# The products with V of each half of the heads, done at two places of the half's eighteen steps instead of four

## What is computed

```
h = _layernorm(x) * (1 + ca) + sa
q, k, v = split(h @ qkv_w.T + qkv_b);  q, k = apply_rope(q), apply_rope(k)
attn = softmax(where(causal, q k^T * scale, -1e9))
x = x + ga * ((attn @ v) @ proj_w.T + proj_b)
h = _layernorm(x) * (1 + cb) + sb
x = x + gb * spikes(square(relu(h @ W_fc.T)) @ W_proj.T)
```

## Time and profile before

| | before |
|---|---|
| three executions, us | 456.43, 461.63, 460.37 |
| the profiled execution, us | 458.5 |
| its span in the trace, us | 456.8 |
| PE busy | 391.4 us (86%) |
| DVE busy | 322.9 us (71%) |
| ACT busy | 260.0 us (57%) |
| mean granted TensorE clock | 0.989 |

### The profile page before, as it was taken

One profiled execution on the slowest core, in us unless ns is written; L12 is line 12 of the kernel. 1 busy time (PEld: TensorE's weight loads), 2 busy tenths in 40 slices (PEclk: granted clock), 3 DMA queues, 4 the chain that ended last, 5 costly groups with the idle time before them and its releaser, 6 DMA issues.

```text
span 456.8 us, 15637 instructions
## 1 busy us (share of the span) xinstructions
PE 391.4 (86%) x6611; PEld 252.2 (55%) x6611; DVE 322.9 (71%) x722; ACT 260.0 (57%) x449; POOL 124.3 (27%) x159
## 2 busy tenths in 40 slices
PE   3768979878999998899989989999899899878882
PEld 2226755545656665576557655766466657445532
DVE  5669858957883998479965996599839845530745
ACT  7202346576577566665695568666675666477220
POOL 7725002421351143304340325133510400220210
PEclk9899999999999999999999999999999999899998
DMA  6055723242314242323324251415141410110000
GB/s 207 23 171 143 234 75 104 67 123 70 112 57 122 71 108 62 101 80 93 89 83 114 52 136 61 130 28 140 52 126 45 113 46 5 27 30 23 24 1 24
DMA packets 26048, 38.53 MB, mean 84 GB/s; under 512 B 5794, under 2 KB 20714, under 8 KB 23690
## 3 DMA queue, kind: packets, MB, share of 16 engines
q1 hardware_dynamic: 25978, 37.53, 28.7%
HBM read 26.35 MB, written 8.65 MB: 77 GB/s over the span
## 4 chain that ended last, share of the span: by engine, by line
PE 44%; DVE 17%; DMA 13%; ACT 8%; SPq 7%; issue 7%; POOL 2%; POOLq 0%; ACTq 0%; DVEq 0%
PE d_bank L448 10%; PE o_bank L519 9%; PE t_bank L501 6%; PE s_bank L468 6%; DMA den<-o_raw 5%; SPq L370 4%; DVE negmax L828 4%; DMA kf<-k_scr 3%; ACT probs L703 3%; PE a_bank L448 3%; DMA rden<-r_scr 2%; DVE rot_s L864 2%; DVE xn L844 2%; SPq L374 2%; DVE count L895 2%
## 5 line engine op out<-in xcount | busy, mean ns | idle before, releaser
L828 DVE TENSOR_REDUCE negmax<-s_bank 128x1 f32<-128x448 f32 (+7 forms) x368 | 192.0, 564 | 69.0 <-PE s_bank L474 67.5
L703 ACT ACTIVATE probs<-t_bank 128x512 f32<-128x512 f32 x288 | 163.4, 595 | 85.8 <-PE t_bank L506 79.5
L468 PE MATMUL s_bank<-kf,qf 126*64 126x448 bf16 (+7 forms) x1024 | 117.4, 292 | 18.4 <-DVE negmax L828 11.7
L501 PE MATMUL t_bank<-qf,kf 128*64 128x512 bf16 (+7 forms) x1024 | 112.8, 290 | 11.6 <-ACT probs L703 10.9
L468 PEld LDWEIGHTS s_bank<-kf,qf 126*64 126x64 bf16 x1024 | 49.7, 110 | 50.2 <-DVE negmax L828 28.5
L519 PE MATMUL o_bank<-probs,v 128*32 128x512 f32 (+7 forms) x1024 | 76.2, 416 | 0.0
L474 PE MATMUL s_bank<-causal,identb 128*64 128x64 bf16 x1024 | 72.5, 194 | 0.0
L506 PE MATMUL t_bank<-causal_t,identb 128*64 128x64 bf16 x1024 | 64.7, 195 | 0.0
L501 PEld LDWEIGHTS t_bank<-qf,kf 128*64 128x64 bf16 x1024 | 41.4, 111 | 32.0 <-ACT probs L703 14.2
L506 PEld LDWEIGHTS t_bank<-causal_t,identb 128*64 128x64 bf16 x1024 | 48.0, 111 | 9.2
L474 PEld LDWEIGHTS s_bank<-causal,identb 128*64 128x64 bf16 x1024 | 47.4, 111 | 8.4 <-issue 8.1
(11 more groups left out here) (115 smaller groups left out, 432.6 us busy)
## 6 DMA issues: line engine op xcount, KB each, us to landing
qf<-q_scr SPq DMA_DIRECT2D x15, 576.0 KB
kf<-k_scr SPq DMA_DIRECT2D x45, 192.0 KB
q_scr<-parts SPq DMA_DIRECT2D x24, 128.0 KB, 1.7
k_scr<-parts SPq DMA_DIRECT2D x24, 128.0 KB, 1.7
xa<-in_x SPq DMA_DIRECT2D x8, 256.0 KB, 4.0
o_t<-o_raw SPq DMA_DIRECT2D x60, 32.0 KB, 2.1
rden<-r_scr SPq DMA_DIRECT2D x15, 128.0 KB
out_y<-count SPq DMA_DIRECT2D x7, 256.0 KB, 7.6
```

The source lines that it names most:

```text
L468: nc.tensor.matmul(bank[C * a:C * (a + 1), col:col + keys], qf[0:KS, slot, 2 * p + a, C * i:C * (i + 1)], kf[0:KS, slot, 2 * p + a, 0:keys ...
L501: nc.tensor.matmul(bank[C * a:C * (a + 1), col:col + w], kf[0:KX, slot, 2 * p + a, C * kb:C * (kb + 1)], qf[0:KX, slot, 2 * p + a, C * kb: ...
L703: nc.scalar.activation(probs[:, v, :], t_bank[u % 2][:, :], ACT.Exp, scale=SCALE).then_inc(e_done, 1)
L828: last = nc.vector.tensor_reduce(own[:, i, p:p + len(same)], cols, AX.X, ALU.max, negate=True)
```

## The change

Two tables of places are rewritten. The blocks 0, 1 and 7 are no longer visited after slot 9 but together with 2 and 6 after slot 13; the late blocks 3 and 5 no longer after slot 0 of the next half but together with 4 after its slot 1. The order of the blocks among themselves, and with it which one starts and which one ends the sum, is as it was.

```diff
-PV_AFTER = {9: (0, 1, 7), 13: (2, 6)}
-PV_LATE = {0: (3, 5), 1: (4,)}
+PV_AFTER = {13: (0, 1, 7, 2, 6)}
+PV_LATE = {1: (3, 5, 4)}
```

## The result

The changed kernel takes 480.94 us (median of 4 executions, 477.86 to 483.54), the kernel before 458.98 us in the same comparison: a ratio of 1.046, 95% interval 1.040 to 1.052. It is 22 us slower. The forecast was 472 us with a range of 463 to 482, so the direction and the range held, and the middle was 9 us too low.

The account below looks back on a forecast made before the run. DVE was taken to pace even slots 5 to 13, PE slots 14 to 17, a DMA chain odd slots 0 to 9. Terms 7.0 + 3.6 + 0.9 + 0.6 = 12.1 us on 460.37 gave 472 us, range 463 to 482.

Parts of the forecast that it names:

- the likeliest case: Slot 13 fixed by DVE or the DMA chain, its longer visit paid, at most two clock falls: 466 to 477 us, chance 0.60.
- the rival in which the clock falls: Waits of 2.7 us before odd halves' query and key product bring half clock, 1.7 us each, six times: 478 to 486, chance 0.17.
- DVE is the pace in slots 5 to 13 of even halves: DVE busy 8.80 of 8.80 us, so slot 13 ends where it did and the removed 1.95 us become PE idle time.
- the sign: Expected in the new trace: PE idle about 1.9 us more between slots 9 and 13 of an even half, ended by DVE.
- The longer visit after slot 13 is paid in even halves: Slots 14 to 17: visit 1.71 us longer, only 0.12 us of the stretch idle, so about 1.6 us stay per even half.
- give-back of 0.2 us at the late visit: Slots 0 to 4 after an even half: PE is the pace, and one saved edge pair gives -0.2 us.
- ACT absorbs about half behind slot 13 of odd halves: Behind slot 13 of odd halves: of the visit's 1.71 us extra, ACT absorbs half, leaving +0.8 us a half.
- The saved edges: 31 fewer visits, each saving two tile-width changes of 0.10 us: 6.2 us less if PE were the bound everywhere.
- Head and tail: Halves 0, 13 and 14 put at 0, half 2 at +0.9 us, half 15 at +0.6 us.
- That PE is the pace: Slots 9 to 13: if DVE's work can go earlier, up to 6.2 us gained: 454 to 456 us, chance 0.08.
- that most is absorbed: Odd halves' shorter PE waits and slack in the `den` DMA absorb most; 5 us or less: 461 to 465 us, chance 0.15.

Follow-up runs that it names:

- DVE light: Four of five spike counts of batches 0 to 6 on 32 columns instead of 512: kernel before 455.44 us, changed kernel 470.14 us.
- the even halves alone: Kernel before with blocks 0, 1, 7 moved from after slot 9 to after slot 13 in even halves only: 470.84 us, ratio 1.024.
- The runs without falls: Changed kernel plus useless repeat products after slot 9, of blocks 0, 1, 7 (480.39 us) or of 0, 7 outside halves 13 and 15 (476.71 us).
- second profile: The kernel before, unchanged, profiled once more: span 456.3 us.
- the short copy: Changed kernel plus useless repeat products of blocks 0 and 7 after slot 9, except in halves 13 and 15: 476.71 us, ratio 1.035.
- the full copy: Changed kernel plus useless repeat products of blocks 0, 1 and 7 after slot 9 of each half: 480.39 us, ratio 1.045.

## Why the forecast was right, and where it was off

The direction and the two costs of the moved visit came out as worked out, half by half. The size did not: 12.1 us were forecast and 22.0 measured. The time lies outside the band of the likeliest case (466 to 477 us) and inside that of the rival in which the clock falls (478 to 486 us, chance 0.17). That the stated range still holds it, by 1 us, is in part luck, because the range took in only the lower part of that rival.

**DVE is the pace in slots 5 to 13 of even halves: right.** The stretch kept its length to 0.1 us while PE's work in it shrank, and with DVE light the cost of an even half fell from 1.4 to 0.5 us. PE's waits for DVE in the stretch grew by 1.4 us (0.6 to 2.0), where about 1.9 was given as the sign.

**The longer visit after slot 13 is paid in even halves: right.** 1.73 us longer (5.02 to 6.75) where 1.6 was forecast. With the give-back of 0.2 us at the late visit, 1.4 us a half was forecast, and even halves without a fall are 1.4 us longer (24.37 against 22.94). With the even halves alone and the late visits as before it is 1.65 us (24.59), where 1.6 was to be expected.

**ACT absorbs about half behind slot 13 of odd halves: right.** 0.8 us forecast, 0.63 measured (6.52 to 7.15). Counted from the start of the window, the copy of the maxima starts 0.49 us later and the ReLU 0.60 us later than before, where 0.45 and 0.55 were forecast; in half 5:

```profile
190.71 1.00 ACT L709 COPY mrow<-a_bank 8x1024 bf16<-8x1024 bf16 x1 [0.39 <-PE a_bank L488]
191.72 0.60 ACT L742 ACTIVATE relu<-d_bank 128x512 f32<-128x512 f32 x1
```

The sum over halves 4 to 12 was 7.0 for five even halves and 4 x 0.8 - 0.6 = 2.6 us for four odd ones, 9.6 us. The runs without falls gave 8.9 and 10.4 us. The saved edges are seen as well: line 519 is busy 71.5 us instead of 76.2 with 31 visits fewer, 4.7 us where 6.2 were worked out, with part of its products at half clock.

**The clock: the mis-sized term.** The forecast gave it 0 in the likeliest case and 10 us in a rival with a chance of 0.17: "if such a wait brings a stretch at half clock". It did, in both kinds of half of the profile, and the four executions have a mean clock of 0.957 to 0.969, where 13 of the kernel before have 0.984 to 0.992. The price of one was 1.7 us in the rival and 1.3 to 1.6 us in the runs. In halves 4 to 12 four falls account for 5.0 to 6.5 of the 15.4 us. The rival's place was too narrow: it counted odd halves alone, but the even halves have falls too, one with the even edit alone and one in half 8 of the changed kernel. There PE waits for DVE in several pieces (the last three are 0.50, 0.19 and 0.46 us), and the clock falls in the last of them, at 263.59:

```profile
263.60:267.00 3.40, 3.22 (x24) 1.36 (x28) 3.32 (x13) 1.01 (x2) 0.51 (x1) 0.50 0.47 120
```

What argued against it, "only one wait did this", was weak evidence, because between 40 us and the end the kernel before has only two waits over 1.5 us, 2.90 us in half 0 and 1.55 us in half 14, and one of the two brought a fall.

**Head and tail: too small.** I had put halves 1 to 3 at 1.9 us together, halves 13 and 14 at 0 and 15 at 0.6 us. The part behind half 12 grew from 98.7 us (96.7 in the second profile) to 103.6 us, and the part before half 4 from 141.1 (143.2) to 146.1 us. PE's waits there were not worked out one by one. Between the first profile of before and that of the changed kernel it is 25.0 - 15.1 = 9.9 us. Both parts hold falls, seven in the changed kernel and three and two in the profiles of before; at 1.3 to 1.6 us each, four or five more would be 5 to 8 us (an estimate). One of the seven follows a wait of 2.54 us in half 2 for the `kf` DMA. How much is the moved work itself stays open; the head differs by 2 us between two profiles of the same kernel.

**The rivals on the other side fell.** That PE is the pace (454 to 456 us) and that most is absorbed (461 to 465 us) are refuted by the 480.94 us and by the stretches. The part of the forecast that the late edit is worth 0.2 us a visit was not confirmed in the times.

## What to carry to other kernels

An engine at 86% busy is not the pace everywhere. Cut one steady period at the points where the full engine changes, and read a moved piece of work as free where it leaves a stretch that another engine fills (or that ends at a DMA chain), and as paid where it arrives. Then ask what the engine does in the time that the work left behind: if it is TensorE, a wait may cost more than itself, because here most waits of 2.3 to 2.8 us, and some shorter ones, were followed by half clock.

## What the runs showed of the hardware

At the second query and key products of the changed kernel, waits of PE of 2.3 to 2.8 us were followed by 3.41 us at half clock in four cases of five, and one of 1.7 us was not. In half 8 a row of waits of 0.2 to 0.5 us was. The wait of 1.55 or 1.56 us in half 14 was followed by a fall in the first profile of before and in that of the changed kernel, and not in the second profile of before. So the length of a wait alone did not tell whether the clock would fall. A fall cost 1.3 to 1.8 us. Useless matmuls in such waits kept the clock at full speed over nine halves (1.00 against 0.97), and the kernel with the short copy was 4.2 us faster than the one with none; with the full copy the total stayed the same (480.39 against 480.94 us). The Trainium skill ("TensorE: Matmul & The Clock Gate", Part 1) describes the throttled clock as the default, from which activity frees the engine; here the trace agrees, with those 0.97 and 1.00. Fillers ahead of the long wait in half 0 of the kernel before did not help; that wait was still 3.13 us long behind them.

Between tiles 64 and 32 columns wide the next matmul started 0.07 us before the last one's end, against 0.17 us between equal widths. 31 visits fewer made line 519 4.7 us less busy.
